# Last pass of a spline layer: deltas added to the result in DRAM by indirect DMAs, cell chain run once for all tiles

## Chip, cores and metric

The kernel runs on one core of one Trainium2 chip, as one program. The metric is the device time of an execution in microseconds, the median of several runs. Times inside an execution come from the profile of one of them.

## What is computed

Four layers follow each other on a tensor of 2 x 4096 rows of 512 columns (8192 tokens): a selective-scan (Mamba) block, a sum of eight matrices applied as one, a linear attention with decay in chunks of 128, and a layer of splines. Only the last concerns this change:

```python
xf = normalised rows, 8192 x 512, 64 tiles of 8 columns
tile_idx = argmax(tile_scores among the best cluster's tiles)      # per token
x_slice = the 8 columns of xf that belong to tile_idx
mn, mx = min and max of x_slice over all tokens of that tile       # per tile, over all tokens
u = clip((x_slice - mn) / (mx - mn + 1e-08), 0.0, 1.0 - 1e-06)
gi = clip((u * GRID).astype(int32), 0, GRID - 1)                    # GRID = 16 cells
b = spline_bases[tile_idx[:, None], j, gi]
s = spline_slopes[tile_idx[:, None], j, gi]
delta = (b + s * (u - gi / GRID) * GRID) * output_scale[tile_idx][:, None]
return x + zeros.at[token, columns of tile_idx].set(delta)
```

The extremes mn and mx need all tokens before the first delta can be made. That splits the layer in two: choosing tiles and gathering extremes, and then a last pass over all tokens.

## The kernel before

`mamba_block` is the first layer. `blocks_after` holds the other three. It first loads and splits weights, with constants loaded by ScalarE's queue (`w_loaded2`), for all of which VectorE waits. Then it walks over 64 row tiles of 128 tokens in a software pipeline written out by hand: in step t each engine does its part of tiles t, t−1 ... t−6. SyncE's queue loads x1t, stores r_t (x of the last layer with its residual, the result without deltas) to `out` and, for the last pass, `ohx`: for each token a one-hot of its tile (64 numbers) and its 8 picked columns. VectorE's functions `score_products` to `keep_extremes` choose the tile of tile t−6, mark it (`mark_tile`, L1351), mask and pick its columns (`mask_dims`, `pick_dims`) and keep the largest and the negated smallest value of each tile in `acc` (128 partitions x 2 x 64).

`finish` is the last pass. After a barrier the extremes are reduced over the partitions: `acc` is transposed by TensorE, reduced by VectorE, and spread to all partitions by a product with ones. Then come 16 groups of four row tiles, on two sets of buffers. SyncE loads the four tiles of `out` (1 MB, into x_all or scm) and of `ohx_d` (into vv). TensorE transposes the one-hots (L1806), ScalarE copies them out of PSUM (L1719), TensorE multiplies them with the tables of bases and slopes (L1812). VectorE looks up the extremes (L1738: one-hots times extremes, L1742: the sums), runs the chain from value to cell (L1746 to L1768, 32 columns a partition, with a drain between any two), compares cells with the grid (L1770), weighs and sums the looked-up tables (L1774, L1778), forms the delta, and spreads it over 2048 columns:

```python
nc.vector.tensor_tensor(od[:].rearrange("p t (i j) -> p t i j", j=DS),
                        oh.unsqueeze(3).to_broadcast([P, N, NTILE, DS]),
                        bsel[:].unsqueeze(2).to_broadcast([P, N, NTILE, DS]), ALU.mult)
```

GpSimd adds that to the loaded tiles (L1710), and SyncE stores them (L1691). In the trace's names, x_all and scm are R, decay is od, qk_all is prod, x1t is eq, kTs holds the small buffers, junk is ohTs.

## Time and profile before

| | before |
|---|---|
| median of 3 runs (lowest, highest) | 5543.72 us (5543.46, 5544.86) |
| profiled execution, its own time | 5545.57 us |
| span of the profile | 5543.6 us |
| TensorE busy | 4955.6 us, 89% |
| VectorE busy | 4611.2 us, 83% |
| GpSimd busy | 3148.7 us, 57% |
| ScalarE busy | 2636.9 us, 48% |

The span runs from the first to the last instruction of the profiled execution. A busy share is a mean over three stages (first block to about 3830 us, second block to 5288.5, last pass to the end), so it tells little of one of them; a stage is read from its own window. PE is TensorE, DVE VectorE, ACT ScalarE, POOL GpSimd, SPq and ACTq are the DMA queues of SyncE and ScalarE. PEclk is the granted TensorE clock, 1.00 is 2.4 GHz and 0.50 is 1.2 GHz.

### The profile page before, as it was taken

The numbers are of one execution on the slowest core, as the hardware profiler recorded it, in microseconds if no ns is written. First come the engines' busy times: TensorE is split into PE (matmuls) and PEld (weight loads), VectorE is DVE, ScalarE is ACT, GpSimd is POOL, SyncE is SP. The second block draws the span as 40 slices with busy tenths as digits, with TensorE's granted clock in tenths as the row PEclk, the third lists the DMA queues.
The fourth block names the chain that finished last, engine by engine and source line by source line (L and its number), as shares of the span: only waits on it lengthen the run. The fifth ranks groups of instructions, "written<-read, shape, count | busy, mean of one in ns | idle before, by whom it ended". The sixth has DMA issues, their size and how long they took to land. (4 is left out here: it accounts for less than half of the span.)

```text
span 5543.6 us, 108449 instructions
## 1 busy us (share of the span) xinstructions
PE 4955.6 (89%) x41157; PEld 2941.5 (53%) x41157; DVE 4611.2 (83%) x7532; ACT 2636.9 (48%) x4244; POOL 3148.7 (57%) x1611
## 2 busy tenths in 40 slices
PE   6899999999999999999999999974899999999922
PEld 3354444454445444454444444432688888888822
DVE  3988889888898888988889888884688888888888
ACT  3655656556565565655656556551233333333300
POOL 1676766767667676676766767662244444434323
PEclk9999999999999999999999999987899999999955
DMA  2222222212222222222222222223110000101034
GB/s 82 81 96 73 100 79 90 96 73 100 81 89 96 73 100 84 85 97 73 100 85 85 96 73 100 81 88 133 37 31 28 29 29 28 31 26 31 22 124 140
DMA packets 139999, 422.20 MB, mean 76 GB/s; under 512 B 38368, under 2 KB 39904, under 8 KB 106592
## 3 DMA queue, kind: packets, MB, share of 16 engines
q1 hardware_dynamic: 136672, 411.75, 21.1%
q8 instruction: 337, 5.52, 0.4%
q10 hardware_dynamic: 2816, 3.51, 0.2%
q14 instruction: 174, 1.43, 0.1%
HBM read 361.99 MB, written 53.22 MB: 75 GB/s over the span
## 5 line engine op out<-in xcount | busy, mean ns | idle before, releaser
L335 POOL TENSOR_TENSOR s<-s,Cb 128x1024 f32<-128x1024 f32 x1024 | 2395.0, 2360 | 1081.9 <-DVE state L656 1070.4
L651 DVE TENSOR_TENSOR_SCAN s<-s,state,BU 128x512 f32<-128x512 f32 x2048 | 2452.9, 1260 | 423.4 <-PE BU L737 387.1
L501 ACT ACTIVATE s<-dt,ch 128x512 f32<-128x512 f32 x2048 | 1305.6, 712 | 776.3 <-PE Y L754 774.7
L754 PE MATMUL Y<-s,ident 64*64 64x512 f32 x8192 | 1010.7, 609 | 78.5 <-POOL s L335 77.6
L683 PE MATMUL PJ<-xnT,w_in 128*128 128x512 f32 x2048 | 946.9, 606 | 9.0 <-ACT dtuT L367 5.7
L737 PEld LDWEIGHTS BU<-spread,dtuT 32*128 32x128 f32 x16384 | 512.4, 189 | 528.8 <-DVE s L651 403.2
L737 PE MATMUL BU<-spread,dtuT 32*128 32x128 f32 x16384 | 610.9, 286 | 146.4 <-DVE s L651 141.0
L683 PEld LDWEIGHTS PJ<-xnT,w_in 128*128 128x128 f32 x2048 | 370.1, 190 | 479.0 <-issue 424.2
L754 PEld LDWEIGHTS Y<-s,ident 64*64 64x64 f32 x8192 | 279.1, 134 | 572.8 <-issue 535.2
L728 PE MATMUL PJ<-w_out,u 128*128 128x512 f32 x1024 | 471.7, 604 | 8.3 <-ACT xnT L371 6.7
L728 PEld LDWEIGHTS PJ<-w_out,u 128*128 128x128 f32 x1024 | 184.5, 189 | 242.9 <-issue 225.3
L1103 POOL TENSOR_TENSOR x1t<-x1t,bias_b 128x512 f32<-128x512 f32 x64 | 82.8, 1294 | 397.4 <-DVE xa L1286 397.4
L544 DVE SCALAR_TENSOR_TENSOR u<-hid,ch,u 128x512 f32<-128x512 f32 x384 | 287.6, 749 | 19.1
L694 PE MATMUL PJ<-w_xp,u 128*128 128x160 f32 x1024 | 253.0, 404 | 9.6 <-issue 6.5
L694 PEld LDWEIGHTS PJ<-w_xp,u 128*128 128x128 f32 x1024 | 243.1, 329 | 27.2 <-issue 20.8
L1108 POOL TENSOR_TENSOR xf<-xf,gamma_b 128x512 f32<-128x512 f32 x64 | 81.5, 1273 | 305.3 <-DVE xf L1475 305.3
L1484 DVE TENSOR_TENSOR scm<-bank,decay 128x512 f32<-128x512 f32 x256 | 159.0, 684 | 71.1 <-PE bank L1593 71.1
L1554 PE MATMUL bank<-w_high_o,aTs 128*128 128x512 f32 x512 | 179.9, 412 | 0.0
L1116 POOL TENSOR_TENSOR qk_all<-rc,rs 128x512 f32<-128x512 f32 x64 | 82.1, 1283 | 172.1 <-DVE rs L1502 172.1
L367 ACT COPY dtuT<-PJ 128x512 f32<-128x512 f32 x128 | 68.8, 587 | 231.8 <-PE PJ L723 231.8
L1554 PE MATMUL bank<-w_high_f,xaT 128*128 128x512 f32 x512 | 177.1, 407 | 1.5 <-DVE xaT L1291 1.4
L1291 DVE TENSOR_TENSOR xaT<-bank,xaT 128x512 fp32r<-128x512 f32 x64 | 44.2, 691 | 161.2 <-ACT xaT L1158 161.2
(219 smaller groups left out, 7171.7 us busy)
## 6 DMA issues: line engine op xcount, KB each, us to landing
Cb<-bc SPq DMA_DIRECT2D x256, 1024.0 KB, 4.8
res<-in_x SPq DMA_DIRECT2D x64, 256.0 KB, 4.8
x<-res SPq DMA_DIRECT2D x64, 256.0 KB, 5.0
x1t<-x SPq DMA_DIRECT2D x64, 256.0 KB, 2.6
out<-r_t SPq DMA_DIRECT2D x64, 256.0 KB, 2.0
xt<-in_x SPq DMA_DIRECT2D x31, 512.0 KB, 5.7
x_all<-out SPq DMA_DIRECT2D x16, 512.0 KB, 4.2
scm<-out SPq DMA_DIRECT2D x16, 512.0 KB, 4.6
```

Of the source, the lines that this page charges most:

```text
L335: nc.gpsimd.tensor_tensor(pair, pair, Cb[q % 2][:, 2 * part * T:2 * part * T + 2 * T], ALU.mult).then_inc(z_ready, 1)
L501: nc.scalar.activation(s[k % SLOTS][:, n, :], dt[p % 2][:, gi, :], ACT.Exp, scale=ch[:, 2 * p + gi, 7 + 4 * nq + n:8 + 4 * nq + n]).then_i ...
L544: last_ = nc.vector.scalar_tensor_tensor(out, h_[:, tap:tap + T], ch[:, m, tap:tap + 1], out, ALU.mult, ALU.add)
L651: nc.vector.tensor_tensor_scan(s[k % SLOTS][:, n, :], s[k % SLOTS][:, n, :], BU[:, n::4], state[:, b, k, n:n + 1], ALU.mult, ALU.add).then ...
L683: last_ = nc.tensor.matmul(bank[:], w_in[:, kb, lo:lo + P], xnT[:, kb, :], start=(kb == 0), stop=(kb == KB - 1))
L694: last_ = nc.tensor.matmul(bank[:, tb % 2 * SP_:(tb % 2 + 1) * SP_], by_block(u[slot][:, g, :])[:, tb], w_xp[:, g, :], start=(g == 0), sto ...
L728: last_ = nc.tensor.matmul(bank[:], u[slot][:, g, j * P:(j + 1) * P], w_out[:, g, :], start=(g == 0), stop=(g == G - 1))
L737: last_ = nc.tensor.matmul(BU[:, i * T:(i + 1) * T].rearrange("p (t b n) -> p b t n", b=TB, n=4)[:, tb], dtuT[rows, gi, tb, :], spread[row ...
L754: last_ = nc.tensor.matmul(Y[r][y_rows(r, gi), :], ident[rows, rows], s[(k_even + gi) % SLOTS][rows, n, :], start=False, stop=(n == 3 and ...
L1103: nc.gpsimd.tensor_tensor(x1t[s_][:], x1t[s_][:], bias_b[:], ALU.add).then_inc(S["x1b_ready"], 1)
L1484: nc.vector.tensor_tensor(scm[:, r, :, :].rearrange("p k n -> p (k n)"), bank(f"sc{r}")[:], decay[:, r, :, :].rearrange("p k n -> p (k n)" ...
L1554: last_ = nc.tensor.matmul(b_[:], src[part][:, k, :], wt, start=(k == 0 and i == 0), stop=(k == KB - 1 and i == 2))
```

## The change

The one-hots stay on chip, as bf16, for all 64 tiles (`oh_all`), and so do the picked columns (`xs_all`); `ohx_d` and its stores and loads are gone. In `finish` nothing of `out` is loaded. TensorE turns all one-hots (products with a bf16 identity), ScalarE copies them to SBUF as f32 (`ohT`, 16 tiles in each of four buffers), and TensorE looks up the two extremes of each token by products of two columns. The chain from value to cell runs once, on 512 columns for all tiles. What is left per group is the comparison with the grid, the weighing and summing of the looked-up tables and the delta. VectorE also computes for every token the number of its 8-column cell in `out`, and GpSimd issues 64 indirect DMAs that add 128 deltas of 8 numbers each to those cells in DRAM.

```diff
--- in blocks_after
-        ohx = [sb(f"ohx{i}", [P, NTILE + DS]) for i in range(2)]
+        oh_all = sb("oh_all", [P, TILES, NTILE], BF16)
+        xs_all = sb("xs_all", [P, TILES, DS])
+        row_base = sb("row_base", [P, TILES])
+        tile_no = sb("tile_no", [P, NTILE])
...
-        ohx_d = nc.dram_tensor("ohx_d", (TILES, P, NTILE + DS), F32, kind="Internal").ap()
...
-                    held(S["ohx_ready"], num(a) + 1)
-                    sp.dma_start(ohx_d[num(a)], ohx[s_][:]).then_inc(ohx_stored[s_], 16)
...
-                             (tie8, w["tie8"]), (tie64, w["tie64"]), (grid16, w["grid16"]), (oscale, w["oscale"])):
+                             (tie8, w["tie8"]), (tie64, w["tie64"]), (grid16, w["grid16"]),
+                             (row_base, w["row_base"]), (tile_no, w["tile_no"]), (oscale, w["oscale"])):
...
-            dve.wait_ge(S["w_loaded2"], 16 * 16)
+            dve.wait_ge(S["w_loaded2"], 16 * 18)
...
             def mark_tile(a):
                 scored_to(a, 9)
-                if a[0] is not None or a[1] >= 2:
-                    dve.wait_ge(ohx_stored[a[1] % 2], 16 * stored_count(a))
...
             def mask_dims(a):
                 scored_to(a, 10)
-                nc.vector.tensor_tensor(xm[:], xf[a[1] % 2][:].rearrange("p (i j) -> p i j", j=DS),
+                by_tile = xf[a[1] % 2][:].rearrange("p (i j) -> p i j", j=DS)
+                nc.vector.tensor_tensor(by_tile, by_tile,
--- the last pass, new (the old one is printed above)
+def finish(nc, out, buf, NTILE, DS, GRID, TILES):
+    N = 4
+    GROUPS = TILES // N
...
+    out_cells = out.rearrange("b s (i j) -> (b s i) j", j=DS)
+    def ohT(t, n=1):
+        per = TILES // 4
+        lo = t % per * P
+        return buf["ohT"][t // per][:, lo:lo + n * P]
+    def per_dim(ap):
+        return ap.rearrange("p (t j) -> p t j", j=DS)
...
+        block = ctx.enter_context(nc.Block())
+        @block.gpsimd
+        def _(pool):
+            pool.wait_ge(rows_ready, 1)
+            for t in range(TILES):
+                if t % N == 0:
+                    pool.wait_ge(delta_ready, t // N + 1)
+                nc.gpsimd.indirect_dma_start(out_cells, bass.IndirectOffsetOnAxis(ap=rows[:, t:t + 1], axis=0),
+                                             delta[:, t * DS:(t + 1) * DS], None, compute_op=ALU.add
+                                             ).then_inc(scattered, 16)
+            pool.wait_ge(scattered, 16 * TILES)
+        @block.scalar
+        def _(act):
+            nc.scalar.copy(ident_b[:], ident[:]).then_inc(ident_ready, 1)
+            for g in range(GROUPS):
+                act.wait_ge(oh_turned, g + 1)
+                nc.scalar.copy(ohT(g * N, N), banks[g % 2][0:NTILE, :]).then_inc(ohT_ready, 1)
+        @block.vector
+        def _(dve):
+            dve.wait_ge(acc_turned, 1)
+            nc.vector.tensor_reduce(ext_T[:], banks[7][:, 0:P], AX.X, ALU.max).then_inc(ext_column, 1)
+            half = TILES // 2
+            for h in range(2):
+                nc.vector.tensor_tensor(
+                    marked[h][:].rearrange("p k (t i) -> p (k t) i", i=NTILE), oh[:, h * half:(h + 1) * half, :],
+                    buf["tile_no"][:].unsqueeze(1).to_broadcast([P, half, NTILE]), ALU.mult).then_inc(marked_ready, 1)
+            dve.wait_ge(ext_full, 1)
+            nc.vector.tensor_copy(ext[:], banks[6][0:NTILE, 0:2]).then_inc(ext_ready, 1)
+            for h in range(2):
+                dve.wait_ge(marked_ready, h + 1)
+                nc.vector.tensor_reduce(idx[:, h * half:(h + 1) * half],
+                                        marked[h][:].rearrange("p k (t i) -> p (k t) i", i=NTILE), AX.X, ALU.add
+                                        ).then_inc(idx_step, 1)
+            dve.wait_ge(idx_step, 2)
+            nc.vector.tensor_tensor(rows[:], idx, buf["row_base"][:], ALU.add).then_inc(rows_ready, 1)
+            steps = itertools.count(1)
+            def then(ins):
+                n = next(steps)
+                ins.then_inc(chain, 1)
+                dve.wait_ge(chain, n)
+            def spread(ap):
+                return ap.unsqueeze(2).to_broadcast([P, TILES, DS])
+            dve.wait_ge(e_full, 1)
+            then(nc.vector.tensor_copy(e, banks[6][:, 0:2 * TILES]))
+            e_q = e.rearrange("p (t q) -> p t q", q=2)
+            then(nc.vector.tensor_tensor(rdn, e_q[:, :, 0], e_q[:, :, 1], ALU.add))
+            then(nc.vector.tensor_scalar_add(rdn, rdn, 1e-8))
+            nc.vector.tensor_tensor(per_dim(v16[:]), xs[:], spread(e_q[:, :, 1]), ALU.add)
+            then(nc.vector.reciprocal(rdn, rdn))
+            then(nc.vector.tensor_tensor(per_dim(v16[:]), per_dim(v16[:]), spread(rdn), ALU.mult))
+            then(nc.vector.tensor_scalar(v16[:], v16[:], 0.0, 1.0 - 1e-6, ALU.max, ALU.min))
+            then(nc.vector.tensor_scalar(v16[:], v16[:], float(GRID), None, ALU.mult))
+            then(nc.vector.tensor_copy(gi[:], v16[:]))
+            then(nc.vector.tensor_copy(gf[:], gi[:]))
+            then(nc.vector.tensor_tensor(gt[:], gf[:], v16[:], ALU.is_gt))
+            then(nc.vector.tensor_tensor(gf[:], gf[:], gt[:], ALU.subtract))
+            then(nc.vector.tensor_tensor(v16[:], v16[:], gf[:], ALU.subtract))
+            def of(ap, g):
+                return ap[:, g * N * DS:(g + 1) * N * DS]
+            def cells(ap):
+                return ap.rearrange("p (c g) -> p c g", g=GRID)
+            def mark(g):
+                if g >= 2:
+                    dve.wait_ge(prod_ready, 2 * (g - 2) + 2)
+                nc.vector.tensor_tensor(cells(eq[g % 2][:]), of(gf, g).unsqueeze(2).to_broadcast([P, N * DS, GRID]),
+                                        grid16[:].unsqueeze(1).to_broadcast([P, N * DS, GRID]), ALU.is_equal
+                                        ).then_inc(eq_ready, 1)
+            def weigh(g, q):
+                if q == 0:
+                    dve.wait_ge(eq_ready, g + 1)
+                    dve.wait_ge(looked_up, g + 1)
+                if g >= 1:
+                    dve.wait_ge(picked, 2 * (g - 1) + 1 + q)
+                nc.vector.tensor_tensor(prod[q][:], eq[g % 2][:], banks[2 * (g % 2) + 2 + q][:], ALU.mult
+                                        ).then_inc(prod_ready, 1)
+            def pick(g, q):
+                dve.wait_ge(prod_ready, 2 * g + 1 + q)
+                if g >= 2:
+                    dve.wait_ge(delta_ready, g - 1)
+                nc.vector.tensor_reduce(sel[:, g % 2, q, :], cells(prod[q][:]), AX.X, ALU.add).then_inc(picked, 1)
+            def slope(g):
+                dve.wait_ge(picked, 2 * g + 2)
+                nc.vector.tensor_tensor(sel[:, g % 2, 1, :], sel[:, g % 2, 1, :], of(v16, g), ALU.mult
+                                        ).then_inc(sloped, 1)
+            def offset(g):
+                dve.wait_ge(sloped, g + 1)
+                nc.vector.tensor_tensor(of(delta, g), sel[:, g % 2, 0, :], sel[:, g % 2, 1, :], ALU.add
+                                        ).then_inc(delta_ready, 1)
+            mark(0)
+            for g in range(GROUPS):
+                if g + 1 < GROUPS:
+                    mark(g + 1)
+                weigh(g, 0)
+                if g > 0:
+                    slope(g - 1)
+                weigh(g, 1)
+                pick(g, 0)
+                if g > 0:
+                    offset(g - 1)
+                pick(g, 1)
+            slope(GROUPS - 1)
+            offset(GROUPS - 1)
+        @block.tensor
+        def _(pe):
+            nc.tensor.transpose(banks[7][:, 0:P], acc[:].rearrange("p q i -> p (q i)"), ident[:]).then_inc(acc_turned, 1)
+            pe.wait_ge(ident_ready, 1)
+            for g in range(GROUPS):
+                if g >= 2:
+                    pe.wait_ge(ohT_ready, g - 1)
+                for t in range(g * N, (g + 1) * N):
+                    last_ = nc.tensor.matmul(banks[g % 2][0:NTILE, t % N * P:(t % N + 1) * P], oh[:, t, :], ident_b[:],
+                                             start=True, stop=True)
+                last_.then_inc(oh_turned, 1)
+                if g == 1:
+                    pe.wait_ge(ext_column, 1)
+                    for q in range(2):
+                        last_ = nc.tensor.matmul(banks[6][0:NTILE, q:q + 1], ident[:, q * NTILE:(q + 1) * NTILE],
+                                                 ext_T[:], start=True, stop=True)
+                    last_.then_inc(ext_full, 1)
+            pe.wait_ge(ext_ready, 1)
+            pe.wait_ge(ohT_ready, GROUPS)
+            for t in range(TILES):
+                last_ = nc.tensor.matmul(banks[6][:, 2 * t:2 * t + 2], ohT(t), ext[:], start=True, stop=True)
+            last_.then_inc(e_full, 1)
+            for g in range(GROUPS):
+                if g >= 2:
+                    pe.wait_ge(prod_ready, 2 * (g - 2) + 2)
+                for q in range(2):
+                    for t in range(N):
+                        last_ = nc.tensor.matmul(banks[2 * (g % 2) + 2 + q][:, t * P:(t + 1) * P], ohT(g * N + t),
+                                                 tab[:, q, :], start=True, stop=True)
+                last_.then_inc(looked_up, 1)
```

The instruction order shows the change on the engines of the last pass; line numbers are those of each kernel. VectorE before, from the end of one group's chain to the next group's first operations (names as above):

```order
L1768 TENSOR_TENSOR kTs<-kTs 128x32
L1770 TENSOR_TENSOR x1t<-kTs,grid 128x512
L1772 ISA
L1774 TENSOR_TENSOR qk_all<-x1t,bank 128x512 [waits looked_up]
L1774 TENSOR_TENSOR qk_all<-x1t,bank 128x512
L1778 TENSOR_REDUCE kTs<-qk_all 128x32 x2
L1781 TENSOR_TENSOR kTs<-kTs 128x32
L1783 TENSOR_TENSOR kTs<-kTs 128x32
L1787 TENSOR_TENSOR decay<-vv,kTs 128x2048 [waits out_ready]
L1738 TENSOR_TENSOR qk_all<-vv,kTs 128x256 [waits oq_loaded1]
L1738 TENSOR_TENSOR qk_all<-vv,kTs 128x256
```

VectorE after, two groups of the loop (xa is eq, xb is prod, x_1 the cells, x_0 the values, kTs the sums, rc the deltas):

```order
L1750 TENSOR_TENSOR xa<-x_1,grid 128x512 [waits prod_ready]
L1760 TENSOR_TENSOR xb<-xa,bank 128x512 [waits picked,looked_up,eq_ready]
L1771 TENSOR_TENSOR kTs<-kTs,x_0 128x32 [waits picked]
L1760 TENSOR_TENSOR xb<-xa,bank 128x512 [waits picked]
L1767 TENSOR_REDUCE kTs<-xb 128x32 [waits prod_ready]
L1776 TENSOR_TENSOR rc<-kTs 128x32 [waits sloped]
L1767 TENSOR_REDUCE kTs<-xb 128x32 [waits prod_ready]
L1750 TENSOR_TENSOR xa<-x_1,grid 128x512 [waits prod_ready]
L1760 TENSOR_TENSOR xb<-xa,bank 128x512 [waits picked,looked_up,eq_ready]
L1771 TENSOR_TENSOR kTs<-kTs,x_0 128x32 [waits picked]
L1760 TENSOR_TENSOR xb<-xa,bank 128x512 [waits picked]
```

The spreading over 2048 columns, the extremes' products and the wait for loaded one-hots are gone, and the small operations of the group before stand between the large ones. TensorE before, from the first product of the pass to the end of its second group:

```order
L1796 MATMUL bank<-ident,acc 128x128
L1798 MATMUL bank<-kTs,ones 128x128
L1806 MATMUL bank<-ident,vv 64x128 x4
L1812 MATMUL bank<-tab,junk 128x128 x8
L1806 MATMUL bank<-ident,vv 64x128 x4
L1812 MATMUL bank<-tab,junk 128x128 x8
```

TensorE after, the whole pass (x1t is the identity in bf16 at L1803 and the extremes at L1815; x_all, qk_all, scm and decay hold the turned one-hots):

```order
L1796 MATMUL bank<-ident,acc 128x128
L1803 MATMUL bank<-x1t,oh_all 64x128 x8
L1809 MATMUL bank<-x1t,ident 64x1 x2
L1803 MATMUL bank<-x1t,oh_all 64x128 x56
L1815 MATMUL bank<-x1t,x_all 128x2 x16
L1815 MATMUL bank<-x1t,qk_all 128x2 x16
L1815 MATMUL bank<-x1t,scm 128x2 x16
L1815 MATMUL bank<-x1t,decay 128x2 x16
L1822 MATMUL bank<-tab,x_all 128x128 x32
L1822 MATMUL bank<-tab,qk_all 128x128 x32
L1822 MATMUL bank<-tab,scm 128x128 x32
L1822 MATMUL bank<-tab,decay 128x128 x32
```

All turning (L1803) now precedes all lookups, with the lookup of the extremes (L1815) between them. GpSimd before, the first groups and the loop's body:

```order
L1710 TENSOR_TENSOR x_all<-x_all,decay 128x2048 [waits r_loaded0,od_ready]
L1710 TENSOR_TENSOR scm<-scm,decay 128x2048 [waits r_loaded1,od_ready]
L1672 UNCONDITIONAL_BRANCH
L1672 ISA
L1709 ISA [waits od_ready]
L1710 TENSOR_TENSOR x_all<-x_all,decay 128x2048 [waits r_loaded0]
L1708 REGISTER_ALU
L1710 TENSOR_TENSOR scm<-scm,decay 128x2048 [waits r_loaded1,od_ready]
```

GpSimd after, the last eight of its 64 indirect DMAs:

```order
L1683 DMA out<-rc,x1t 524288x8 [waits delta_ready]
L1683 DMA out<-rc,x1t 524288x8 x3
L1683 DMA out<-rc,x1t 524288x8 [waits delta_ready]
L1683 DMA out<-rc,x1t 524288x8 x3
L1663 UNCONDITIONAL_BRANCH [waits scattered]
```

The additions of 2048 columns are gone, and GpSimd's queue holds DMAs alone, four behind each wait for deltas.

## Rows read from the trace of the kernel before

**Rows 1.** Stages: us, PE, PEld, DVE, ACT, POOL busy (x instructions), PEclk, DMA share, GB/s.
```profile
4600.00:5200.00 600.00, 592.93 (x4656) 496.39 (x4659) 504.57 (x1437) 196.44 (x456) 245.08 (x198) 1.00 0.09 28
5288.50:5543.60 255.10, 78.21 (x323) 65.04 (x323) 215.86 (x387) 9.25 (x16) 73.81 (x16) 0.50 0.41 141
```

**Rows 2.** Timeline, one group of the last pass: start, us, engine, line.
```profile
5376.54 1.29 DVE L1774 TENSOR_TENSOR qk_all<-x1t,bank 128x512 f32<-128x512 f32 x2
5377.95 1.28 DVE L1778 TENSOR_REDUCE kTs<-qk_all 128x32 f32<-128x512 f32 x2
...
5379.83 2.29 DVE L1787 TENSOR_TENSOR decay<-vv,kTs 128x2048 f32<-128x2048 f32 x1
...
5381.93 1.03 PE L1806 MATMUL bank<-ident,vv 128*64 128x128 f32 x4 [9.05 <-DMA vv<-ohx_d]
5382.04 5.08 DVE L1738 TENSOR_TENSOR qk_all<-vv,kTs 128x256 f32<-128x256 f32 x2
5382.20 4.63 POOL L1710 TENSOR_TENSOR scm<-scm,decay 128x2048 f32<-128x2048 f32 x1 [10.78 <-DVE decay L1787]
5383.00 0.58 ACT L1719 COPY junk<-bank 64x512 f32<-64x512 f32 x1 [13.95 <-PE bank L1806]
...
5383.63 3.77 PE L1812 MATMUL bank<-tab,junk 64*128 64x128 f32 x16 [0.67 <-ACT junk L1719]
...
5390.15 0.19 DVE L1764 TENSOR_TENSOR kTs<-kTs 128x32 f32<-128x32 f32 x1
5390.42 0.19 DVE L1766 TENSOR_TENSOR kTs<-kTs 128x32 f32<-128x32 f32 x1
...
5391.63 1.29 DVE L1774 TENSOR_TENSOR qk_all<-x1t,bank 128x512 f32<-128x512 f32 x2 [0.15 <-issue]
```

**Rows 3.** Line L1738: duration in ns min/median/max, first and last start.
```profile
L1738 DVE TENSOR_TENSOR qk_all<-vv,kTs x32: 410/426/4774, 5295.2 to 5523.8; 128x256 f32<-128x256 f32 x32
```

**Rows 4.** DMA in 5288 to 5544: packets, MB, share; issues, KB, median us to landing.
```profile
q1 hardware_dynamic: 25856, 35.92, 41.2%
...
out<-scm SPq DMA_DIRECT2D x16, 512.0 KB, 3.2
vv<-ohx_d SPq DMA_DIRECT2D x16, 144.0 KB, 4.6
```

**Rows 5.** DMA issues of the whole execution: count, KB, median us to landing.
```profile
ohx_d<-ohx SPq DMA_DIRECT2D x64, 36.0 KB, 1.5
...
rot<-in_rot SPq DMA_DIRECT2D x64, 16.0 KB, 1.8
```

**Rows 6.** Timeline, end of the second block's loop and first product of the last pass.
```profile
5286.16 0.29 DVE L1379 TENSOR_TENSOR acc<-acc,cand 128x128 f32<-128x128 f32 x1
5286.18 0.33 SPq L1081 DMA_DIRECT2D ohx_d<-ohx  x1
...
5288.55 0.45 PE L1796 MATMUL bank<-ident,acc 128*128 128x128 f32 x1 [22.12 <-PEq L1633]
```

**Rows 7.** Timeline, constants of the second block and VectorE's first operation.
```profile
3841.11 0.63 ACTq L1146 DMA_DIRECT2D tab<-in_slopes  x1
...
3848.02 0.28 DVE L1236 TENSOR_REDUCE smean<-tab 64x8 f32<-64x128 f32 x1 [19.16 <-DMA tab<-in_slopes]
```

**Rows 8.** Timeline, sums of squares on TensorE.
```profile
5247.01 1.05 PE L1570 MATMUL bank<-ones,junk 128*128 128x1 f32 x8 [1.28 <-ACTq L1228]
```

**Rows 9.** TensorE at the second block's start: timeline, then stages as in rows 1.
```profile
3900.64 1.09 PE L1544 MATMUL bank<-ident,xa 128*128 128x128 f32 x4 [49.26 <-DVE xa L1286]
...
3905.00:3910.00 5.00, 3.54 (x13) 2.63 (x11) 1.57 (x3) 0.19 (x2) 1.27 (x1) 0.77 0.01 2
...
3915.00:3920.00 5.00, 5.00 (x24) 4.13 (x23) 2.49 (x6) 0.79 (x2) 1.29 (x1) 1.00 0.16 52
```

**Rows 10.** Line L1286, a one-input operation on 512 columns: ns min/median/max.
```profile
L1286 DVE TENSOR_SCALAR xb<-x_all,mv_b,rd_b x64: 534/540/550, 3910.2 to 5217.8; 128x512 f32<-128x512 f32 x64
```

**Rows 11.** Timeline, SyncE's last two stores.
```profile
5538.94 0.89 SPq L1691 DMA_DIRECT2D out<-scm  x2
```

More of the change, by code:

```diff
@@ L1 @@
+import itertools
 import numpy as np
@@ L962, in blocks_after @@
         pr = sb("pr", [P, HID], BF16)
-        xm = sb("xm", [P, NTILE, DS])
         ts = sb("ts", [P, NTILE])
@@ L1030, in blocks_after @@
         r_stored = [sem(f"r_stored{i}") for i in range(2)]
-        ohx_stored = [sem(f"ohx_stored{i}") for i in range(2)]
         var_ready = {n: sem(f"var_ready_{n}") for n in ln}
@@ L1813, in body @@
                                                  tab[:, q, :], start=True, stop=True)
                 last_.then_inc(looked_up, 1)
-            groups(pe, body)
 def constants():
```

175 lines of the change are left out of this document (28 added, 147 removed).

## The prediction, made before the changed kernel ran

> **What bounds the kernel now.** I read the busy time by stage first [rows 1]. From 4600 to 5200 us, in the main loop of the second block, TensorE works 592.93 of 600 us: that stage is TensorE's, and what VectorE or a queue gains there can hardly show. The last pass, from 5288.5 to 5543.6 us, is 255 us long, 4.6% of the span. VectorE is busy for 216 of them, TensorE for 78, ScalarE for 9, and TensorE's granted clock is 0.50, the lower level (1.2 GHz).
>
> Next, one group of that pass in the timeline [rows 2]. From one L1774 (5376.54) to the next (5391.63) are 15.1 us; sixteen of them make 242, the pass. Where do they go? The lookup proper, L1774 and L1778, takes 1.3 us each. The cell chain is ten small operations that start 0.26 or 0.27 us apart (L1764, L1766). L1787 spreads the deltas over 2048 columns in 2.29 us. Then L1738 of the next group starts at 5382.04 and lasts 5.08 us for a pair, though one of it can take 0.410 [rows 3]. It lies beside GpSimd's L1710 (5382.20, 4.63 us): the two exclude each other, so 16 × 4.6 = 74 us of GpSimd's addition stand in VectorE's path. TensorE's lookup (3.77 us) and ScalarE's copy (0.58) hide beside that. The pass is bound by VectorE with GpSimd in series, and not by transfers (41.2% of the DMA engines) [rows 4].
>
> **What goes.** The pass is replaced whole: 32 MB of loads and stores, L1738, L1787, L1710, and fifteen of sixteen runs of the chain. So I build the new one from its start.
>
> **The start.** Before, the last store of ohx_d is issued at 5286.18; it lands 1.5 us later [rows 5, 6], and the first product of the pass stands at 5288.55, 0.87 after the landing. Without the store the pass can begin 0.87 us after VectorE's last operation (5286.16 + 0.29), at 5287.3: 1.2 us earlier. Against it, ScalarE issues two more constant loads ahead of tab's, for whose landing VectorE's first operation waits [rows 7]. An issue there costs up to 0.63 us, two 1.3 if the landing follows the issue, 0 if the megabytes ahead of it set it; I take 0.8. In the main loop 64 small stores and a wait for them go, and the one-hot is bf16: the same operations on the same columns, beside a TensorE that is 99% busy, so nothing. If that cover were gone, 0.1 us a tile would be 6 us. The pass begins at 5288.55 − 1.2 + 0.8, about **5288.1**.
>
> **Turning the one-hots.** 64 bf16 products, and a ScalarE copy of 64x512 after each four, on two banks. The copy is 0.58 us; four f32 transposes at the low clock were 1.03 [rows 2]. So 0.6 to 1.03 a group. A bf16 product reads half the bytes, so I take the copy's pace: 0.5 + 16 × 0.6 + 0.6 = 10.7 us, to 5298.8 (at 1.03, 7 us later). Beside it VectorE makes the row numbers: two products like L1787 (2.29), two reductions of four times L1778's single (4 × 0.64) and small ones, 10.6 us. TensorE goes on without it, and Pool needs the rows much later; if not covered, it would be those 10.6.
>
> **Extremes by TensorE.** 64 products of two columns; an f32 product leaves two records (L1812 shows 16 for 8), so 128. L1570, eight records with a moving operand of one column, took 1.05 us at the high clock [rows 8], 0.131 each; L1812 at the low one 3.77 / 16 = 0.236. So 16.8 or 30.2 us. Which? In the last pass TensorE works 1.03 + 3.77 us of every 15 and stays at 0.50. At the block's start it first works at 3900.64, shows 0.77 between 3905 and 3910 and 1.00 after 3915 [rows 9]. Here it pauses for no longer than a copy, so I take the high one and keep 13.4 us for the range. Ready at 5315.6.
>
> **The chain, once for all tiles.** 13 operations on up to 512 columns: a PSUM copy of 128 (0.29 as L1379, which has as many columns [rows 6]), five two-input ones at 0.68, four one-input ones at 0.54 [rows 10], three narrow at 0.18: 6.4 us, and twelve hand-overs of 0.07 (0.26 from start to start less 0.19 busy). 7.2 us, to 5322.8, and nothing covers it.
>
> **Sixteen groups of cells.** Each is a comparison, two weighings and two reductions at 0.64, and two small ones: 3.5 us of VectorE. TensorE's lookup for it is 16 records, 2.1 us at the high clock and 3.8 at the low, two groups ahead; at the low one TensorE would set 3.8 a group, 5 us in all. The first deltas stand after a group and most of the next, 6.8 us: 5329.6. The last at 5380.
>
> **64 indirect DMAs that add.** No row shows one. Each takes 128 cells of 32 bytes (read, add, write). Pool's queue holds nothing else; behind the wait for the first deltas all 64 are queued, and only the end of the program waits for them. From below: SyncE issues a small transfer in 0.33 us [rows 6], and then they would keep up with the deltas (four in 3.5 us, 0.87 each). By the DMA engines: 25856 packets in 41.2% of 16 × 255.1 us are 65 ns a packet; eight cells an engine, each read and written, 1.0 us. From above, with reading, writing and issuing in series: rot's small load 1.8, ohx_d's store 1.5, issue 0.33, 3.6 us. I take **1.5 us**, the row nearest in form (128 short rows from SBUF to DRAM [rows 5]), as Pool's pace: 96 us, to 5425.6. Behind it a landing of 1.5 and what stood behind the last landing before: second store issued at 5539.4, 3.2 to landing, end 5543.6, so 1.0 [rows 4, 11]. 5428.1.
>
> By the Trainium skill (DMA: Bandwidth & Descriptors, section Anatomy of one DMA — SWDGE) such a DMA has about 2.0 us of fixed cost; if they didn't overlap, an estimate by it is 64 × 2.0 and an end at 5460. No run here shows that yet.
>
> Will the making of descriptors on GpSimd and VectorE's operations exclude each other, as L1738 and L1710 do (0.41 against 5.08)? In the group loop the comparison and the two small operations have two inputs in SBUF, 1 us of 3.5. If they did, Pool would lose 15 × 1 us while the deltas are made: 5443. The Trainium skill (SBUF — State Buffer, the box on the "DVE blocks DMA" trap) says that GpSimd can't write descriptors while VectorE runs a one-input operation in its two-port mode, and lets two-input ones pass; the loop has no such operation, and the chain's casts are over by then, so by it 5428 stands. The trace shows blocking beside additions, and nothing yet of descriptors.
>
> **The sum.** A span of 5428.1 against 5543.6, minus 115.5. The profiled execution took 5545.57 us; the median of the runs is 5543.72, within 0.2 of the span, so I set time equal to span: **5428 us**, 2.1% less.
>
> **Rivals.**
> - Pool keeps up, at most 0.87 us a DMA, and VectorE sets the end: 5380 + 3.5 + 2.5 = 5386. For it, the issue row of 0.33; against it, 128 addresses are computed for each. 13%.
> - Reading and writing in series, twice 1.5 = 3.0 us a DMA: 5329.6 + 192 + 2.5 = 5524, still 0.4% faster. 8%.
> - The other side: no overlap at all, 3.6 us a DMA. 5329.6 + 232.3 + 2.5 = 5564, slower by 0.4%. For it, 8192 cells of 32 bytes, each a trip to DRAM and back; against it, vv's loads of 512 rows land in 4.6 us [rows 4], 9 ns a row, so rows do overlap. It decides from (5543.6 − 2.5 − 5329.6) / 64 = 3.3 us a DMA. 6%.
> - The clock stays at 0.50: all 13 us later, 5441; it belongs to the forecast's case, as 5443 does.
>
> The forecast's case, 0.9 to 2.8 us a DMA, has 73%.
>
> **How the numbers follow.** A measurement of this kernel tells some 0.2%, 11 us, from no change. The forecast's case, the keeping up and the doubled price are all faster, 0.94, less what lies between 3.1 and 3.5 us a DMA, 0.03 for the same; slower 0.05. So 0.92, 0.03, 0.05. The range begins where VectorE sets the end, 5386, and goes to 5510: 2.6 us a DMA and the low clock (5329.6 + 13.4 + 166.4 + 2.5 = 5512). Beyond it lie the two dear rivals.
>
> **What would show it.** The first indirect DMA near 5330; 3.5 us from comparison to comparison, and no operation of 5 us in the pass; Pool's queue without a gap to the end, its starts 1.5 us apart; the clock at 1.00 while the extremes are looked up. Wrong it would be first by the price of a DMA (0.1 us is 6.4), then by the clock, then by a pace of the turning above 0.6.

## The result, and the profile after

The changed kernel takes 5467.19 us, the median of four runs (5465.47 to 5468.60), beside 5544.29 for the kernel before in the same session (5543.46 to 5545.29): a ratio of 0.986, with a 95% interval of 0.9845 to 0.9874. 5428 was predicted. The profiled execution's own time is 5468.6 us and its span 5466.8.

The stages of the changed kernel (us, then busy us and instructions of PE, PEld, DVE, ACT and POOL, then the granted clock, DMA share and GB/s), the counterpart of [rows 1]:

```profile
4600.00:5200.00 600.00, 592.93 (x4643) 496.69 (x4642) 504.42 (x1435) 196.87 (x457) 245.71 (x198) 1.00 0.09 27
5288.20:5299.60 11.40, 9.49 (x70) 7.02 (x70) 9.36 (x7) 8.79 (x17) 0.00 (x0) 0.50 0.01 2
5299.60:5327.00 27.40, 27.40 (x129) 27.40 (x129) 0.00 (x0) 0.00 (x0) 0.00 (x0) 0.50 0.00 1
5288.00:5467.00 179.00, 92.12 (x453) 89.05 (x453) 67.84 (x132) 8.79 (x17) 100.30 (x64) 0.50 0.15 2
```

The main loop of the second block is what it was: TensorE works 592.93 us of 600. The last pass went from 255 to 179 us. VectorE's 216 us in it are now 68, and GpSimd is busiest, at 100 us where it had 74. The granted clock is 0.50 in all of the pass, also in the third row, where TensorE works 27.40 us of 27.40. It was already at 0.50 when the pass began: TensorE had stood idle for 20.23 us before its first product (next rows), and from 5280 to 5284 the clock reads 0.50.

The timeline of the changed kernel's last pass (start, us, engine, line, and idle time ahead with its releaser):

```profile
5287.62 0.29 DVE L1376 TENSOR_TENSOR acc<-acc,cand 128x128 f32<-128x128 f32 x1
5288.23 0.45 PE L1796 MATMUL bank<-ident,acc 128*128 128x128 f32 x1 [20.23 <-PEq L1630]
...
5292.51 1.12 PE L1803 MATMUL bank<-x1t,oh_all 128*64 128x128 bf16 x8 [0.18 <-ACT qk_all L1693]
5293.19 1.06 ACT L1693 COPY qk_all<-bank 64x512 f32<-64x512 f32 x2 [0.24 <-PE bank L1803]
5293.82 1.11 PE L1803 MATMUL bank<-x1t,oh_all 128*64 128x128 bf16 x8 [0.19 <-ACT qk_all L1693]
...
5299.60 6.95 PE L1815 MATMUL bank<-x1t,x_all 64*128 64x2 f32 x32 [0.76 <-ACT decay L1693]
5306.42 6.96 PE L1815 MATMUL bank<-x1t,qk_all 64*128 64x2 f32 x32
...
5327.07 0.29 DVE L1725 COPY kTs<-bank 128x128 f32<-128x128 f32 x1 [28.96 <-PE bank L1815]
...
5333.82 1.29 DVE L1750 TENSOR_TENSOR xa<-x,grid 128x512 f32<-128x512 f32 x2
...
5339.91 0.18 DVE L1776 TENSOR_TENSOR rc<-kTs 128x32 f32<-128x32 f32 x1
...
5341.04 1.85 POOL L1683 DMA_INDIRECT out<-rc,x1t  x1 [59.63 <-DVE rc L1776]
5343.19 1.55 POOL L1683 DMA_INDIRECT out<-rc,x1t  x1 [0.30 <-issue]
5345.04 1.55 POOL L1683 DMA_INDIRECT out<-rc,x1t  x1 [0.30 <-issue]
...
5451.55 1.55 POOL L1683 DMA_INDIRECT out<-rc,x1t  x1 [0.30 <-issue]
5455.10 1.56 POOL L1683 DMA_INDIRECT out<-rc,x1t  x1 [2.00 <-issue]
...
5460.68 1.55 POOL L1683 DMA_INDIRECT out<-rc,x1t  x1 [0.30 <-issue]
```

So the pass is a series: turning to 5299.6, the extremes to 5327.1, the chain to 5333.8, the first deltas at 5340, and then GpSimd's queue without a wait for anything but its own issue. No operation of 5 us, such as L1738 in [rows 2], is left. All 64 of these DMAs (ns, min/median/max, first and last start), and the page's row of their queue (packets, MB, share):

```profile
L1683 POOL DMA_INDIRECT out<-rc,x1t x64: 1538/1546/2024, 5341.0 to 5460.7; - x64
```

```profile
q0 software_dynamic: 9216, 0.27, 0.5%
```

9216 packets are 144 a DMA, for 128 cells. Each occupies GpSimd for 1.55 us, and 0.30 us of issue lie between two: 1.85 us from one to the next.

### The profile page after: what moved, and what is told of

Same layout as the page of the kernel before. It is cut to its first block and busy times, and to the rows that moved or that the text cites. A ratio compares the mean times of both kernels' runs of the same rounds, so it can differ in the third digit from the quotient of the medians.

```text
span 5466.8 us, 107541 instructions
## 1 busy us (share of the span) xinstructions
PE 4975.0 (91%) x41287; PEld 2967.0 (54%) x41287; DVE 4462.5 (82%) x7277; ACT 2636.9 (48%) x4245; POOL 3175.6 (58%) x1659
## 3 DMA queue, kind: packets, MB, share of 16 engines
q0 software_dynamic: 9216, 0.27, 0.5%
```

## The experiments

The theory after the result had three parts: GpSimd's queue is the bound, at 1.85 us a DMA; the extremes cost 27.45 us because the granted clock stayed low; and the old addition of GpSimd had stood in VectorE's path. The first four kernels are variants of the changed one. e1_write, e2_half_rows, e3_no_dmas, e5_before_few_added, e6_write_half and e7_add_16_rows leave out part of the work and ran once each, so what counts in them are the durations inside the profile. In the four of them that issue indirect DMAs the first starts 2 to 4 us earlier than in the changed kernel (e1_write: 5337.4 against 5341.0), and some 7 us lie behind the last one, where the changed kernel has 4.6; neither was followed up.

### Writing instead of adding, and half the rows

```diff
-   delta[:, t * DS:(t + 1) * DS], None, compute_op=ALU.add
+   delta[:, t * DS:(t + 1) * DS], None                       (e1_write)
-   ap=rows[:, t:t + 1] ... delta[:, ...]
+   ap=rows[0:64, t:t + 1] ... delta[0:64, ...]               (e2_half_rows, still adding)
```

> The changed kernel with its 64 indirect DMAs writing the deltas instead of adding them (the addition is left out). In the changed kernel a DMA of 128 cells starts every 1.85 us on GpSimd. Theory A (GpSimd's own work per DMA, making 128 addresses and descriptors, sets that pace): nothing changes, 1.85 us apart and a time of 5467, within 3 us. Theory B (reading, adding and writing back in DRAM sets it, and holds the queue up): the pace falls towards 1.0 us and the time by up to 50 us, to some 5415 to 5430.

> The changed kernel, each indirect DMA over 64 partitions instead of 128 (half of the deltas are left out). If GpSimd's cost goes by the row, a DMA takes about 0.93 us, GpSimd nearly keeps up with the deltas (0.86 each) and the time is about 5405. If it is a fixed cost per DMA, 1.85 us apart and 5467. Half and half: 1.4 us, 5436.

e1_write took 5428.98 us, e2_half_rows 5455.8. Their rows, of the first and of the second:

```profile
L1683 POOL DMA_INDIRECT out<-rc,x1t x64: 954/959/1472, 5337.4 to 5419.4; - x64
```

```profile
L1683 POOL DMA_INDIRECT out<-rc,x1t x64: 1400/1406/1950, 5336.9 to 5445.5; - x64
```

Writing makes one 0.96 us instead of 1.55, and 1.26 us apart. The expectation that nothing would change fell, and the rival's size (a time of 5415 to 5430) came. Its reason, a queue held up by DRAM, is not what the rows show. The difference lies in the instruction's own duration on GpSimd, and the very first DMA, which has none ahead of it, is already dearer when it adds: 1.85 us against 1.30. The profile also gives the time from issue to landing: 2.1 us in the median when writing, 2.8 when adding 64 rows, and 3.0 when adding 128 (in e4_bf16_extremes, whose DMAs are those of the changed kernel). The next DMA starts 1.26, 1.71 and 1.85 us after its predecessor, so none waits for a landing. The lines for landing (min/median/max), of e1_write, e2_half_rows and e4_bf16_extremes:

```profile
DMA to landing us min/median/max: 2.1/2.1/3.5
DMA to landing us min/median/max: 2.7/2.8/3.4
DMA to landing us min/median/max: 2.9/3.0/4.4
```

What fills GpSimd's time when it adds is open. Half the rows save only 0.14 us: the price is nearly fixed per DMA.

### No DMAs

```diff
-   for t in range(TILES): wait; indirect_dma_start(...)
-   pool.wait_ge(scattered, 16 * TILES)
+   pool.wait_ge(delta_ready, GROUPS)
```

> The changed kernel without its indirect DMAs (no delta reaches the result). It shows where TensorE and VectorE alone would end: VectorE's last delta stands at 5387.7 in the changed kernel, so if GpSimd's DMAs cost VectorE nothing, span and time are about 5390, and VectorE's operations in the loop are 0.68 us as beside the DMAs. If GpSimd's descriptor making and VectorE's two-input operations exclude each other, VectorE's loop is several us shorter here and the time 5375 to 5385.

It took 5388.22 us, where 5390 was expected if the DMAs cost VectorE nothing. From the pass's first product to the end of VectorE's last operation it is 99.50 us (5286.39 to 5385.89), and in the changed kernel 99.51 (5288.23 to 5387.74). The equal length alone would not prove much, since TensorE's look-ups set the loop's pace in its later part (in the changed kernel they run without a pause from 5346.8 to 5384.5). But the operations of VectorE last 0.68 us in both, and the comparisons of the first groups are 3.19 us apart in both. The weighing, without the DMAs (busy time, mean ns) and in the changed kernel (ns, min/median/max):

```profile
L1754 DVE TENSOR_TENSOR xb<-xa,bank 128x512 f32<-128x512 f32 x32 | 21.7, 680 | 1.8 <-PE bank L1816 0.7
```

```profile
L1760 DVE TENSOR_TENSOR xb<-xa,bank x32: 673/680/689, 5335.0 to 5385.3; 128x512 f32<-128x512 f32 x32
```

The other way round it holds too: of GpSimd's DMAs beside the loop three behind the first are longer (1.68, 2.02 and 1.96 us), 1.0 us in all, and the rest take the 1.55 us that they take when VectorE is done. So these DMAs and these operations of VectorE do not exclude each other. The Trainium skill (SBUF — State Buffer, section Who interferes with whom) says the same of `tensor_tensor` and `tensor_reduce`, which did not stall a DMA from GpSimd, and calls its reason inferred; the trace agrees, at 0.68 us with the DMAs and without them.

### The extremes as bf16 products

The extremes are split into three bf16 parts each, whose sum they are, and one bf16 product a tile looks up six columns, whose parts VectorE adds.

```diff
-   matmul(banks[6][:, 2 * t:2 * t + 2], ohT(t), ext[:], ...)
+   matmul(banks[6][:, 6 * t:6 * t + 6], ohT(t).bitcast(BF16)[:, 1::2], ext_parts, ...)
```

> The changed kernel with the extremes looked up in bf16: the upper halves of the turned f32 one-hots are read as bf16 with a step of two, and the extremes are split into three bf16 parts (64 products of six columns, one record each instead of two, plus two additions of 128 columns on VectorE). My theory is that the 27.45 us of these products are on the path, being 128 f32 records 0.215 us apart at the granted clock of 0.50: 64 bf16 records at 0.13 us, as in the turning, make 8.5 us; less 0.6 for the additions, everything behind starts 18.4 us earlier and the time is 5449. Rival 1: reading with a step of two is slow, and the time stays at 5467 or rises. Rival 2: the clock rises with other products and the gain is larger, 5440.

5441.84 us in four runs (5439.0 to 5442.33), ratio to before 0.9813 (0.9797 to 0.9829). Its timeline and its DMAs:

```profile
5297.92 0.56 PE L1830 MATMUL bank<-x1t,x_all 64*128 64x6 bf16 x16 [0.76 <-ACT decay L1695]
...
5314.41 1.85 POOL L1685 DMA_INDIRECT out<-rc,x1t  x1 [34.69 <-DVE rc L1791]
```

The look-up is 1.7 us (5297.92 to 5299.63) instead of 27.45, at the same granted clock of 0.50. That is far below the 8.5 us expected: a record takes 0.027 us, and the 0.13 of the turning was no guide to it. The time lies near the second rival's 5440, but not for its reason, a rising clock. The first DMA starts 26.6 us earlier, and the time falls by 25.4: what stands ahead of GpSimd's queue counts nearly in full.

### What a DMA's price is made of

```diff
+   rows[0:64, ...], delta[0:64, ...], no compute_op          (e6_write_half)
+   rows[0:16, ...], delta[0:16, ...], compute_op=ALU.add     (e7_add_16_rows)
```

> The changed kernel, writing instead of adding, and only the cells of 64 of the 128 rows of a tile (the other rows lack theirs, and the written cells hold the bare delta). Beside the write of 128 rows (0.96 us busy, 1.26 us from one to the next) it splits the price of a write: if a row costs what it costs when adding (2.3 ns, from 1538 ns with 128 rows and 1400 ns with 64), one is busy 0.81 us and they follow at 1.11 us, and the time is about 5419 to 5423 us, since VectorE's last delta at 5387.7 us and the start bound it little. Rival: a row is dearer because the busy time is the writing of descriptors (0.96 us over 128 rows is 7.5 ns each): then 0.48 us busy, 0.8 us apart, and VectorE's pace of 3.43 us a group (0.86 a tile) takes over, about 5395 us.

> The changed kernel, adding only the cells of 16 of the 128 rows of a tile (the other rows lack theirs). From 1538 ns with 128 rows and 1400 ns with 64 a line gives 1262 ns at none and 1297 ns with 16, and with the 0.30 us between them a pace of 1.60 us: about 5449 us. Rival: the price goes with the descriptors or packets (80 a DMA with 64 rows, 144 with 128, so 32 with 16 if there is one extra for each of 16 queues), which gives the same slope; only if a fixed part is bound to each of 16 DMA engines would nothing go below 64 rows, with 1.40 us busy and 5456 us as with 64.

They took 5435.56 and 5450.75 us. With the runs above (packets are the page's row of the queue, over 64):

| one DMA | us on GpSimd | from one to the next | packets |
|---|---|---|---|
| adds 128 rows | 1.546 | 1.85 | 144 |
| adds 64 rows | 1.406 | 1.71 | 80 |
| adds 16 rows | 1.279 | 1.58 | 32 |
| writes 128 rows | 0.959 | 1.26 | 32 |
| writes 64 rows | 0.892 | 1.20 | 32 |

The straight line for adding held (1.297 expected for 16 rows, 1.279 measured). An added row costs 2.2 to 2.6 ns, a written one 1.0, so that the expected 0.81 us of the half write is 0.89, and the rival with 7.5 ns a row is far off. Adding leaves about 1.24 us for no row, writing 0.83, to which 0.30 us of issue come each time. Of 1.85 us, then, 1.54 are paid for no row at all.

The half write's time is above the full one's (5435.56, 5428.98) although its pace is quicker. In its timeline VectorE is idle several times, without a releaser in the profile, for example:

```profile
5351.77 0.69 DVE L1760 TENSOR_TENSOR xb<-xa,bank 128x512 f32<-128x512 f32 x1 [5.11 <-issue]
...
5354.36 0.68 DVE L1750 TENSOR_TENSOR xa<-x,grid 128x512 f32<-128x512 f32 x1
5365.12 0.69 DVE L1760 TENSOR_TENSOR xb<-xa,bank 128x512 f32<-128x512 f32 x1 [10.08 <-issue]
```

A third pause of 12.87 us stands before 5395.80, and TensorE is idle in the same stretches. The changed kernel, e1_write, e2_half_rows and e7_add_16_rows have nothing like it there (0.7 us ahead of all 32 of these operations). GpSimd in turn waits 6.49 and 6.08 us for deltas. Without these 12.6 us the time would be about 5423, an estimate, at the upper end of the 5419 to 5423 expected. Only the duration of its DMAs is used here, and what the pauses are stays open.

The Trainium skill (DMA: Bandwidth & Descriptors, section Anatomy of one DMA — SWDGE) has about 2.0 us of fixed cost for a DMA from GpSimd, and the estimate by it in the prediction was an end at 5460. That page puts most of these 2.0 us in the confirmation that the data have landed, so what compares with it is the time to landing, 2.1 us when writing and 3.0 when adding 128 rows; the pace is another figure, 1.26 and 1.85. The Trainium skill (Perfetto Trace Analysis, section DMA Instruction — SWDGE (GPSIMD)) says that the profile's row of such a DMA ends when the last descriptor is written, not when the data have moved. The traces agree that the row ends before the landing (0.96 us against 2.1, 1.55 against 3.0); that the row is the writing of descriptors no run here shows. Packets alone do not give its length: 32 of them take 1.28 us when adding and 0.89 or 0.96 when writing.

### The kernel before, with GpSimd adding almost nothing

```diff
-   nc.gpsimd.tensor_tensor(R[v][:], R[v][:], od[:], ALU.add)
+   nc.gpsimd.tensor_tensor(R[v][:, 0, 0:8], R[v][:, 0, 0:8], od[:, 0, 0:8], ALU.add)
```

> The kernel before, whose GpSimd adds only 8 of the 2048 columns of a group (the rest of the result lacks its deltas). Theory A, the prediction's: in the old last pass the addition of GpSimd lies in a chain of one group (spread by VectorE, added by GpSimd, stored), and the next spread waits for it through the one buffer of the spread deltas; take the addition's some 4.6 us away and each of 15 groups gives back about 4.2 us (a short operation stays), 63 to 68 us in all: about 5479 us. Theory B: the loads and stores of the 64 tiles set the old pass's pace, and the time stays at 5544 us. In between, at the length of VectorE's own work, lies whatever it has to do that the addition did not already hide.

It took 5481.15 us, beside 5545.6 for the kernel before (5479 expected). One group of it, where [rows 2] has 15.1 us:

```profile
5379.41 1.28 DVE L1774 TENSOR_TENSOR qk_all<-x1t,bank 128x512 f32<-128x512 f32 x2 [0.28 <-PE bank L1812]
...
5385.07 0.20 POOL L1710 TENSOR_TENSOR scm<-scm,decay 128x8 f32<-128x8 f32 x1 [10.56 <-DVE decay L1787]
5385.22 0.76 DVE L1738 TENSOR_TENSOR qk_all<-vv,kTs 128x256 f32<-128x256 f32 x2 [0.22 <-DMA vv<-ohx_d]
...
5390.95 1.28 DVE L1774 TENSOR_TENSOR qk_all<-x1t,bank 128x512 f32<-128x512 f32 x2 [0.62 <-PE bank L1812]
```

L1738 takes 0.76 us a pair instead of 5.08, and a group 11.54: 3.6 less in this one, 4.0 a group in the mean (64.5 over 16). The size was as expected, but the expectation's reason, a wait through the one buffer of the spread deltas, is not what the rows show: L1738 follows L1787 at once in both, and what became short is L1738 itself. It is the exclusion of the prediction's first part: without the neighbour, none of the 32 L1738 takes more than 0.464 us, where the longest had taken 4.774:

```profile
L1738 DVE TENSOR_TENSOR qk_all<-vv,kTs x32: 411/423/464, 5296.5 to 5463.5; 128x256 f32<-128x256 f32 x32
```

The gain is 64.5 us and not the 74 counted there: all 32 L1738 together take 12.2 us instead of 76.3, 64.1 less. The pair of the first group had no addition beside it, and the other fifteen lost 4.3 us each, not 4.6. So this one addition, taken out alone, is worth 64.5 us, and the whole change 77: most of what else the change removes is paid back by its own serial stages and its DMAs.

### TensorE kept busy ahead of the pass

Products that nobody reads, to hold the clock up: behind the second block's last product, and between those of the turning.

```diff
+   for i in range(72):                                       (e9_warm; 92 in e11_warm_longer)
+       nc.tensor.matmul(warm[:], aTs[0][:, i % KB, :], w_high["o"][:, i % KB, :], ...)
    last_.then_inc(oh_turned, 1)
+   nc.tensor.matmul(banks[5][:], *buf["warm"], ...)          (two of them in e9_warm, one in e11)
```

> The changed kernel with products of TensorE added whose results nobody reads: 72 of 128x512 behind its last product of the second block (where it otherwise waits some 20 us for the last sign, and the granted clock falls from 0.83 to 0.50) and two after each four products of the turning. It asks whether the extremes' 27.45 us (128 records, 0.215 apart) are the price of the low clock. Theory A, the prediction's step: they are; with the clock at 1.00 when the look-up begins, and TensorE busy throughout, the look-up takes 16.8 us (0.131 a record), the turning some 1 us more for the added products, and the time is 5467 - 10.7 + 1 = 5457 us. Rival B: the look-up's own products let the clock fall, as it never rose over 80 us of them in the changed kernel: 1.00 at its start, 0.50 soon after, and a time of 5460 to 5468 us. Rival C: the 0.215 us are not the clock's: a granted clock of 1.00 and still 27 us.

> The earlier run with added products left a gap of 5.44 us between the last of them (5280.4) and the pass's first product, behind which the granted clock was 0.50 again, so its look-up of the extremes never ran at the high level. Now 92 instead of 72 unread products of 128x512 stand ahead of the pass (20 more at 0.235 us, 4.7 us, so the gap is under 1 us) and one instead of two behind each four of the turning. Theory A (the low clock is the price of the 27.45 us): the clock is at 1.00 while the turning and the look-up run; the look-up takes 16 to 17 us, the turning stays at ScalarE's pace of 0.65 us a group, and the time is 5467 - 10.7 = 5456 us, less if the lookups of cells gain too. Rival B: without a pause the clock still falls within the pass, by what the pass's products are: a window with TensorE busy at 0.50, and 5467 us plus up to 16 x 0.5 = 8 us for the added products. Rival C: the clock is at 1.00 and the look-up still takes 27 us.

e9_warm took 5472.78 us in four runs (5470.98 to 5483.29; the profiled one is the longest). The gap that remained was enough:

```profile
5263.54 16.90 PE L1631 MATMUL bank<-w_high_o,aTs 128*128 128x512 f32 x72
5285.88 0.45 PE L1800 MATMUL bank<-ident,acc 128*128 128x128 f32 x1 [5.44 <-PEq L1633]
...
5290.14 0.61 PE L1807 MATMUL bank<-x1t,oh_all 128*64 128x128 bf16 x4
5290.68 1.22 PE L1811 MATMUL bank<-w_high_o,aTs 128*128 128x512 f32 x2
```

In the profiled execution the granted clock was 1.00 up to 5283, read 0.78 in the next microsecond of the gap and 0.50 from 5284 on, so that two added products took 1.22 us and the turning 1.72 a group. Its look-up never ran at the high level, and the run did not answer the question. The other three executions are 9 to 12 us shorter, and their mean clock is 0.967 instead of 0.965; there is no trace of them, and they may have gone otherwise. e11_warm_longer, with a pause of 0.87 us, did; 5465.61 us in four runs (5464.38 to 5466.16). Its stages, all engines, then those of the look-up alone (PE, PEld, clock, DMA share, GB/s):

```profile
5286.00:5290.00 4.00, 4.00 (x27) 2.33 (x26) 4.00 (x4) 2.96 (x6) 0.00 (x0) 1.00 0.00 0
5290.00:5295.00 5.00, 5.00 (x33) 2.74 (x34) 3.24 (x3) 3.86 (x7) 0.00 (x0) 1.00 0.01 3
5300.00:5305.00 5.00, 5.00 (x25) 5.00 (x25) 0.00 (x0) 0.00 (x0) 0.00 (x0) 0.50 0.00 0
```

```profile
5296.80:5297.80 1.00, 0.98 (x9) 1.00 (x10) 1.00 0.00 0
5297.80:5298.80 1.00, 1.00 (x10) 1.00 (x9) 0.80 0.00 0
5298.80:5299.80 1.00, 1.00 (x6) 1.00 (x7) 0.50 0.00 0
```

Between them the look-up begins, behind a pause of 0.33 us:

```profile
5296.82 5.51 PE L1820 MATMUL bank<-x1t,x_all 64*128 64x2 f32 x32 [0.33 <-ACT decay L1697]
5302.20 6.96 PE L1820 MATMUL bank<-x1t,qk_all 64*128 64x2 f32 x32
```

The clock is 1.00 through the turning and for the look-up's first 1.6 us, and then falls to 0.50 in the midst of it, with TensorE busy all the time from the look-up's start. The first 32 records take 5.38 us to the next 32. At 0.215 us each, the 3.8 us at the low clock hold 17.7 of them, which leaves 14.3 for the first 1.6 us, an estimate of 0.11 us a record at the high clock. The look-up as a whole is 26.0 us (5296.82 to 5322.8). So rival C is out: the pace does follow the clock, and at the high level throughout the look-up would be some 14 us, by the same estimate. The low clock is thus about half of the 27.45 us, and products ahead of the look-up did not avoid it, as rival B had it. That these products let the clock fall is the nearest reading, but not shown: TensorE also paused for 0.87 us before the pass and for 0.33 us just before the look-up, and no run is without these.

### All of the work, shared between GpSimd and VectorE

With the bf16 look-up. The last groups are spread and added by VectorE to rows that SyncE loads and stores, tile by tile, in buffers that the second block no longer needs.

```diff
+   FIRST = GROUPS - 5                            (e8_hybrid; GROUPS - 6 in e10_hybrid_six)
-   for t in range(TILES):                        (GpSimd's DMAs)
+   for t in range(FIRST * N):
+   @block.sync: sp.dma_start(R[k], tile_rows(k)) for each k; later sp.dma_start(tile_rows(k), R[k])
+   nc.vector.tensor_tensor(od[k % 2], oh[:, t, :] spread over 8, delta spread over 64, ALU.mult)
+   nc.vector.tensor_tensor(R[k], R[k], od[k % 2], ALU.add)
```

> All of the work, shared: the look-up of the extremes is in 64 bf16 products as in the earlier run (5441.8 us), and the last 5 of the 16 groups are not given to GpSimd but spread and added by VectorE to rows of the result that SyncE has loaded meanwhile (20 tiles, one DMA of a tile's 128 rows of 512 elements in, one out). If the pace of GpSimd's DMAs, 1.85 us each and nearly all of it fixed, is what bounds the end, 20 DMAs less give back 37 us: first DMA at 5314.4 us, 44 of them end at 5396.5 us, 4.7 us of tail, 5401 us of span and 5403 us of time. VectorE then has 40 operations of about 0.68 us more, 27 us behind the last offset at about 5361 us, so it ends at 5388 to 5390 us and its last store at about 5393 us, just short of GpSimd. Rival: VectorE and GpSimd or the loads, stores and adding DMAs hinder each other; then the DMAs' pace or VectorE's 0.68 us grows, and the time stays above 5415 us.

> As the shared version (5406.8 us), with six of the 16 groups for VectorE instead of five (24 tiles; the rows of the last four go into buffers that are free once the first four are stored). If GpSimd's DMAs still set the end, four less at 1.85 to 1.9 us give back 7.5 us: about 5399.5 us. VectorE's last addition stood at 5386.4 us with five groups, 13 us ahead of GpSimd's last DMA, so 5.5 us more for it are covered: it ends at 5392 us, its last store lands about 5395 us. Rival: the two last ends have met because stores and adding DMAs hinder each other, and the gain is under 3 us.

e8_hybrid: 5406.84 us in four runs (5406.11 to 5407.49), ratio 0.975 (0.9734 to 0.9767). e10_hybrid_six: 5399.67 in five (5396.24 to 5403.9), ratio 0.9739 (0.9725 to 0.9752), the fastest kernel of this study; its median is 7.2 us below e8_hybrid's, where 7.5 were expected. The end of the latter's timeline:

```profile
5376.65 2.24 POOL L1712 DMA_INDIRECT out<-rc,x1t  x1 [0.30 <-issue]
5376.78 0.69 DVE L1838 TENSOR_TENSOR qdT<-qdT,junk 128x512 f32<-128x512 f32 x1
5377.49 0.33 SPq L1703 DMA_DIRECT2D out<-qdT  x1
...
5385.84 0.68 DVE L1838 TENSOR_TENSOR kd<-kd,x1t 128x512 f32<-128x512 f32 x1
5385.95 0.94 SPq L1703 DMA_DIRECT2D out<-kd  x2
5387.64 1.54 POOL L1712 DMA_INDIRECT out<-rc,x1t  x1 [0.30 <-issue]
```

Both ends have met: VectorE's last addition at 5385.84, GpSimd's last DMA at 5387.64. e8_hybrid came out 3.8 us above its 5403: its 44 DMAs take 1640 ns in the mean (median 1545), up to 2.24 us while SyncE's stores and VectorE's additions run beside them, and 1.54 again from 5387.5 on, when VectorE is done. That is some 4 us above the median (the 64 of the changed kernel are 1.4 above theirs), and which of the two neighbours makes it was not tried.

## Why the prediction was right, and where it was wrong

The time lies inside the range, and the forecast's case is the one that came: GpSimd's queue sets the end, at a price a DMA between 0.9 and 2.8 us. The forecast was 38.7 us of span too low (5428.1, 5466.8). Term by term:

| step | predicted | measured | difference |
|---|---|---|---|
| begin of the pass | 5288.1 | 5288.2 | 0.1 |
| turning | 10.7 | 11.4 | 0.7 |
| extremes | 16.8 | 27.5 | 10.7 |
| chain | 7.2 | 6.75 | -0.45 |
| to the first DMA | 6.8 | 7.2 | 0.4 |
| 64 DMAs | 96 | 121.2 | 25.2 |
| behind them | 2.5 | 4.6 | 2.1 |

- **What bounds the kernel now** was right, and e5 shows it: without the long addition, 64.5 us less. The 74 counted for it was too much: fifteen additions stood in the path, not sixteen, at 4.3 us each. The main loop did not move (592.93 us of 600 in both).
- **The start** is right by luck. VectorE's last operation to the first product went from 2.10 us [rows 6] to 0.32, 1.8 us gained instead of 1.2. The two more loads cost 0.4 us instead of 0.8 (from the first constant's issue to VectorE's first operation it is 16.56 us before and 16.95 after), and the second block from there to VectorE's last operation was 0.6 us shorter. Against all that, the first block ended 1.7 us later in the profiled execution, which the change does not touch.
- **Turning** follows ScalarE's copies, as taken: 1.30 us for two groups, 0.65 each instead of 0.6.
- **Extremes by TensorE** is the step whose reason failed. It said that the clock would be at 1.00 because TensorE pauses for no longer than a copy. It left out the pause ahead of the pass, which [rows 6] shows at 22.12 us, so that the pass began at 0.50, and the clock did not rise though TensorE was then 100% busy for 27.4 us. e11 shows that a look-up that begins at 1.00 loses it within 2 us all the same. "It belongs to the forecast's case", the working said of the low clock, with 13.4 us kept for it; 10.7 it was, at 0.215 us a record instead of 0.236. The high clock's 0.131 from L1570 was too dear as well, by the estimate of 0.11 from e11.
- **The chain** was as long as summed in its operations, 6.43 us against 6.4, but by errors that cancel: four one-input operations took 0.43 us and not the 0.54 of L1286 [rows 10], and the reciprocal 0.55 and not 0.18. It came out shorter by its hand-overs, 0.03 or 0.04 us each instead of 0.07.
- **The groups** are 3.19 us apart at first, and 3.4 from 5357 on, where TensorE's look-ups at the low clock have no pause left: the price of that clock put at 3.8 a group is 3.43, and GpSimd's queue covers it.
- **64 indirect DMAs** is the term that was mis-sized: 1.85 us a DMA for 1.5, which makes 22.4 of the 25.2 us; the rest are DMAs of 1.7 to 2.0 us and one pause of 2.00 at 5453, ahead of the last four (e4 has one of 1.95 at the same place; what it is stays open). The 1.5 came from a row that tells when data land [rows 5]. The real price is time that GpSimd itself is busy, 1.55 us, and 0.30 us of issue. The landing comes later, at 3.0 us in e4, and nothing waits for it until the end of the program; adding 16 rows or 128 differs by 0.27 us. The bounds below (0.87) and above (3.6) held it.
- **Behind them** 4.6 us and not 2.5. If the landing of the last is the 3.0 us of e4 from its issue, that is 1.5 behind the row, as taken, and the program's end costs 3.1 us instead of 1.0, an estimate; no run tells why.
- **No exclusion between descriptors and VectorE**: shown by e3, by durations on both sides. The rivals Pool keeps up and 3.0 or 3.6 us a DMA are excluded by 1.85; a plain write would have been at 1.26, still not at 0.87.

## What to carry to other kernels

An indirect DMA from GpSimd was paid per instruction here, and hardly per row (16 to 128 rows of 32 bytes; longer rows were not tried): count the instructions, look whether its pace (here 1.85 us with an addition, 1.26 without) is below that of what feeds it, and give what exceeds it to an engine that has time left; the best share is where both end together. When a pass is a series of stages ahead of such a queue, each microsecond of a stage counts (26.6 us earlier gave 25.4), so the small serial stage (27 us of two-column products) is worth more than anything beside the queue. And when a long operation appears in a profile with a median of 426 ns and a maximum of 4774 [rows 3], look at what the neighbour engine does: taking out that neighbour's one addition alone gave 64.5 us, five sixths of what the whole change gave.

## What the runs showed of the hardware that was not expected

- The granted clock can be 0.50 with TensorE 100% busy: 27.4 us of 64x2 f32 products, and the cell look-ups up to 5380, all at 0.50; with products of 128x512 before it the clock was 1.00, and it fell 1.6 us into the two-column products, with no pause since their start. In e9_warm's profiled execution the clock fell to 0.50 within a pause of 5.44 us, and 28 us of alternating 128x128 and 128x512 products behind it, TensorE busy throughout, did not bring it back. Why is open.
- A product of 64 rows and two f32 columns cost 0.43 us at the low clock (two records of 0.215), one of six bf16 columns 0.027 (64 in 1.7 us): sixteen times.
- An adding indirect DMA shows as many packets as rows and 16 more (144, 80 and 32 for 128, 64 and 16 rows), a writing one 32 for 128 rows as for 64; the addition costs 0.6 us of GpSimd for 128 rows.
- The next of these DMAs starts before the one ahead has landed: 1.85 us from one to the next, 3.0 to landing.
